# A 12-sublayer transformer kernel: L0X without its int16-to-bf16 cast, grouped attention with exponentials one step later, FFN heads merged, and the L3F Hadamard's last stage on TensorE

## The reference

```
        q = _fq_sym(q, axis=-1)          # k likewise; v along the keys
        attn = jnp.einsum('bhqd,bhkd->bhqk', q, k)
        attn = jax.nn.softmax(attn.astype(jnp.float32), axis=-1)
        attn = _fq_unsigned(attn, axis=-1)   # round(x / s) in 0..255, s = max / 255
        out = jnp.einsum('bhqk,bhkd->bhqd', attn, v)
```

```
        def weight_quant(w):
            scale = 1.0 / jnp.clip(jnp.mean(jnp.abs(w)), EPS)
            wq = jnp.clip(jnp.round(w * scale), -1.0, 1.0) / scale
        ...
        def h_bitlinear(x, w):   # fwht: Walsh-Hadamard over the 1024 features
            return jnp.einsum('bsh,oh->bso', act_quant(fwht(x)), weight_quant(w))
        intermediate = jax.nn.silu(bitlinear(x, w_gate)) * bitlinear(x, w_up)
        return h_bitlinear(intermediate, w_down)
```

## Time and profile before

| | us |
|---|---|
| Median of 3 runs (lowest, highest) | 3699.54 (3693.35, 3704.68) |
| The profiled execution, and its span | 3698.16, 3696.4 |
| TensorE busy | 3011.3 (81%) |
| VectorE busy | 2610.3 (71%) |
| ScalarE busy | 1861.4 (50%) |
| GpSimd busy | 469.7 (13%) |

### The profile page before, as it was taken

The page is one execution under the profiler, slowest core; times in us unless marked ns, Lnnn a source line. Parts: engine busy times, 40 slices in busy tenths (PEclk is TensorE's granted clock), DMA queues, the critical chain, the costliest instruction groups (busy, mean ns, idle before and its releaser), DMA issues. The chain is left out here.

```text
span 3696.4 us, 55018 instructions
## 1 busy us (share of the span) xinstructions
PE 3011.3 (81%) x16870; PEld 2203.5 (60%) x16888; DVE 2610.3 (71%) x8154; ACT 1861.4 (50%) x5724; POOL 469.7 (13%) x589
## 2 busy tenths in 40 slices
PE   7985564988999999775599855699999999998565
PEld 5653332756777778552277632377777777776354
DVE  4658887348888887668855589667667676775776
ACT  4546675115555555446522234466666666664232
POOL 0002111001111110221111100111111111111100
PEclk9996555989999999886699977799999999998577
DMA  1004555100000000101100131000000000000011
GB/s 61 2 9 91 102 105 119 56 15 1 1 1 1 1 1 1 43 33 20 43 1 1 48 117 29 23 1 1 1 1 1 1 1 1 1 1 36 3 23 43
DMA packets 192417, 96.23 MB, mean 26 GB/s; under 512 B 186112, under 2 KB 190336, under 8 KB 190464
## 3 DMA queue, kind: packets, MB, share of 16 engines
q1 hardware_dynamic: 192128, 92.73, 10.3%
HBM read 44.47 MB, written 2.10 MB: 13 GB/s over the span
## 5 line engine op out<-in xcount | busy, mean ns | idle before, releaser
L2269 ACT ACTIVATE L3A_probs<-L3A_masked,L3A_negmax 128x128 f32<-128x128 f32 (+1 forms) x512 | 229.3, 451 | 222.0 <-DVE L3A_negmax L2320 221.2
L336 PE MATMUL ps<-s_weights_b,s_XT 128*128 128x512 f32 (+1 forms) x640 | 300.7, 600 | 17.0 <-ACT s_XT L759 7.1
L2320 DVE CUSTOM_DVE_ANT_0 L3A_masked<-ps,L3A_hidden,L3A_negrstd 128x128 f32<-128x128 f32 (+1 forms) x512 | 193.7, 415 | 104.1 <-PE ps L2211 80.7
L2239 PE MATMUL ps<-s_weights_b,L3A_OT 128*128 128x256 f32 x1024 | 263.2, 380 | 0.0
L2192 POOL TENSOR_TENSOR L3A_rstd<-L3A_ve,s_mhalf 128x4 f32<-128x4 f32 x144 | 145.1, 1007 | 866.2 <-DVE L3A_ve L2152 866.2
L2176 DVE TENSOR_TENSOR L3A_rot<-ps,L3A_G 128x512 f32<-128x512 f32 x144 | 99.6, 692 | 207.4 <-ACT s_oT L2117 128.4
L885 ACT ACTIVATE L0X_pf<-ps,L0X_bias,L0X_qscale 128x512 int16<-128x512 f32 x256 | 197.0, 777 | 94.0 <-DVE L0X_bias L918 93.5
L336 PE MATMUL ps<-s_weights_b,s_Xc 128*128 128x512 f32 x512 | 241.3, 594 | 0.0
L915 DVE TENSOR_REDUCE L0X_negmax<-ps 128x2 f32<-128x1024 f32 x128 | 156.1, 1220 | 38.8 <-PE ps L826 38.5
L336 PEld LDWEIGHTS ps<-s_weights_b,s_XT 128*128 128x128 f32 x640 | 122.8, 211 | 101.5 <-issue 71.6
L2239 PEld LDWEIGHTS ps<-s_weights_b,L3A_OT 128*128 128x128 f32 x1024 | 175.4, 191 | 13.1
(11 more groups left out here) (510 smaller groups left out, 8298.8 us busy)
## 6 DMA issues: line engine op xcount, KB each, us to landing
s_weights_b<-w_L3A SPq DMA_DIRECT2D x1, 9984.0 KB, 26.8
s_weights_b<-w_L1A SPq DMA_DIRECT2D x1, 7936.0 KB, 21.5
s_weights_a<-w_L2F SPq DMA_DIRECT2D x1, 4224.0 KB, 12.8
s_weights_b<-w_L1F SPq DMA_DIRECT2D x1, 3840.0 KB, 12.1
s_weights_b<-w_L3F SPq DMA_DIRECT2D x1, 3136.0 KB, 11.3
s_weights_a<-w_L2A SPq DMA_DIRECT2D x1, 2898.0 KB, 10.5
s_weights_a<-w_L0F SPq DMA_DIRECT2D x1, 2176.0 KB, 9.8
s_X<-x SPq DMA_DIRECT2D x1, 2048.0 KB, 8.3
```

What stands on the lines that cost most here:

```text
L336: last = pe.matmul(out, lhs(k), rhs(k), start=(k == 0), stop=(k == n - 1))
L2239: last = pe.matmul(c.bank(3)[:, j * DM:(j + 1) * DM], OT[:, u % 4, j * P:(j + 1) * P], w["wo"][:, h, :], start=(h == 0 and j == 0), stop=( ...
L2269: last = a.activation(pr[:, u % 4, cols], ms[:, u % 2, cols], ACT.Exp, bias=nmx[:, h, j:j + 1], scale=-1.0, accum_out=sm[:, h, j:j + 1])
L2320: last = eng.tensor_tensor_reduce(out=ms[:, u % 2, cols], in0=s[:, cols], in1=hidden[:, P - j * P:2 * P], scale=-1.0 if gated else nrs[:, ...
```

## The change

**L0X.** The cast is gone. `pf` has four buffers, the DMA transpose reads it as it is, and PE reads the 16 bits of each whole number as a half-precision float: 0 to 255 are then subnormals, n times 2 to the -24. V is half precision too. A factor 2^-24 goes into the reciprocal of the sums (one more small DVE operation for each sequence). exps(p) now waits for the landing of transpose p-4, and `VALUE_LAG` is 5.

```
-    VALUE_LAG = 6
+    VALUE_LAG = 5
...
-        pf = S.sb("pf", [P, 3, 2, KEYS], I16)
-        ph = S.sb("ph", [P, 4, 2, KEYS], BF16)
-        pT = S.sb("pT", [P, 4, 2, KEYS], BF16)
+        pf = S.sb("pf", [P, 4, 2, KEYS], I16)
+        pT = S.sb("pT", [P, 4, 2, KEYS], I16)
...
-                        sp.wait_ge(vec_stepped, vec_steps(p))
+                    sp.wait_ge(exp_ready, p + 1)
                     if p >= 4:
                         sp.wait_ge(o_made, p - 3)
-                    sp.dma_start_transpose(out=pT[:, p % 4].rearrange("p x (t q) -> p (x t) q", q=P), in_=flat(ph[:, p % 4])).then_inc(
+                    sp.dma_start_transpose(out=pT[:, p % 4].rearrange("p x (t q) -> p (x t) q", q=P), in_=flat(pf[:, p % 4])).then_inc(
...
-                            last = pe.matmul(c.bank(6)[:, j * DM + h * DH:j * DM + (h + 1) * DH], pT[:, p % 4, x, t * P:(t + 1) * P],
+                            last = pe.matmul(c.bank(6)[:, j * DM + h * DH:j * DM + (h + 1) * DH], pT[:, p % 4, x, t * P:(t + 1) * P].bitcast(F16),
...
+                    if p >= 4:
+                        a.wait_ge(turned[p % 4], 16 * (p // 4))
...
-                    v(eng.reciprocal(ri[:], sm[:, b % 2]))
+                    v(eng.tensor_scalar(ri[:], sm[:, b % 2], STEP, None, ALU.mult))
+                    v(eng.reciprocal(ri[:], ri[:]))
...
-                    if 0 <= s - 2 < U and not by_pool(s - 2):
-                        steps_of(s - 2)
```

```
                         take_out(s - 5)
+                    if 0 <= s - 1 < U:
+                        exps(s - 1)
                     for x in early.get(s, []):
                         act_side(a, x)
                     if 0 <= s - 3 < U:
                         take_probs(s - 3)
-                    if 0 <= s < U:
-                        exps(s)
...
+                    if 0 <= s - 2 < U:
+                        normalize(s - 2)
                     if 0 <= s < U:
                         maxima(s)
-                    if 0 <= s - 1 < U:
-                        normalize(s - 1)
```

```
+                for m in (2, 1):
+                    a.activation(flat(Wb[2][:]), parts[m], ACT.Abs, accum_out=tot[:, m:m + 1]).then_inc(last_sums_ready, 1)
+                    a.wait_ge(last_sums_ready, 3 - m)
+                if norms:
+                    a.wait_ge(inv_ready, 1)
+                    a.activation(lnp[:, 0:3], mean[:, 0:3], ACT.Ln, bias=c.ones[:, 0:1]).then_inc(ln_ready, 1)
...
+                    prepare(0)
+                else:
+                    a.activation(warm[:], c.ones[:, 0:1], ACT.Silu)
...
+                    if s == 0:
+                        weights(1)
+                    if s == 2:
+                        weights(2)
```

```
-                    for ch in range(FCH):
-                        last = pe.matmul(c.bank(5 + ch // 4)[:, (ch % 4) * P:(ch % 4 + 1) * P], uT[:, ch, :], w["h128"],
-                                         start=True, stop=True)
+                    for ch in range(FCH // 2):
+                        two = c.bank(5 + ch // 2)[:, (ch % 2) * 2 * P:(ch % 2 + 1) * 2 * P]
+                        pe.matmul(two, uT[:, ch, :], hx[:, 0:2 * P], start=True, stop=False)
+                        last = pe.matmul(two, uT[:, ch + FCH // 2, :], hx[:, P:3 * P], start=False, stop=True)
...
-                    for s in (1, 2, 4):
+                    for s in (1, 2):
```

More of the change, by code:

```diff
@@ L1259, in sublayer_ternary_ffn @@
         hq_turned = S.sem("hq_turned_0", "hq_turned_1")
         parts = [flat(w["w1"]), flat(w["w2"]), flat(w["w3"])]
[L1261 to L1301, removed]
@@ L1302, in sublayer_ternary_ffn @@
-        S.clear()
+        warm = S.sb("warm", [P, 1])
+        nmagic = S.sb("nmagic", [P, 1])
+        count = 1.0 / (F1024 * DM)
         def row(t):
@@ L1457, in input_mean, with input_factor, weights @@
                     v(eng.tensor_scalar(ms[:, t, 0:1], ss[:, t, 0:1], 1.0 / DM, 1e-8, ALU.mult, ALU.add), xmean_ready)
+                def input_factor(t):
+                    b_ = am2[:, t, 0:XQ] if norms else am2[:, t, 0:1].to_broadcast([P, 2])
+                    v(eng.tensor_tensor(f[:, t, 0:2], b_, wsc[:, 0:2], ALU.mult))
+                def weights(m):
+                    part, out = parts[m], flat(Wb[m][:])
+                    if norms:
+                        eng.wait_ge(part_ready, m + 1)
+                        v(eng.tensor_scalar(out, part, MAGIC, MAGIC, ALU.add, ALU.subtract), w_ready, free=True)
+                    elif m == 2:
+                        eng.wait_ge(part_ready, 3)
+                        v(eng.tensor_scalar(out, out, -1.0, 1.0, ALU.max, ALU.min), w_ready, free=True)
+                    else:
+                        if m == 0:
+                            v(eng.tensor_scalar(part, part, inv[:, 0:1], MAGIC, ALU.mult, ALU.add))
+                        else:
+                            eng.wait_ge(part_ready, 1)
+                        v(eng.tensor_scalar(part, part, MAGIC, 1.0, ALU.subtract, ALU.min))
+                        v(eng.tensor_scalar(out, part, -1.0, None, ALU.max), w_ready, free=True)
                 def scale_input(t):
@@ L1569, in norm @@
                                         ALU.subtract, ALU.mult))
+                eng.wait_ge(S.loaded, 16)
+                v(eng.tensor_reduce(tot[:, 0:1], parts[0], AX.X, ALU.add, apply_absolute_value=True), sums_ready, free=True)
                 if norms:
                     input_mean(0)
+                else:
+                    v(eng.memset(nmagic[:], -MAGIC), free=True)
                 scale_input(0)
+                if hadamard:
+                    for k in range(2):
+                        v(eng.tensor_copy(hx[:, k * P:(k + 1) * P], w["h128"]), free=True)
+                    v(eng.tensor_scalar(hx[:, 2 * P:3 * P], w["h128"], -1.0, None, ALU.mult), free=True)
+                eng.wait_ge(sums_made, 1)
+                v(eng.tensor_scalar(mean[:, 0:3], c.bank(0)[:, 0:3], count, None, ALU.mult))
+                if norms:
+                    v(eng.tensor_scalar(wsc[:, 0:3], mean[:, 0:3], 1e-8, None, ALU.add))
+                else:
+                    v(eng.tensor_scalar(wsc[:, 0:3], mean[:, 0:3], 1e-5, None, ALU.max))
+                v(eng.reciprocal(inv[:, 0:3], wsc[:, 0:3]), inv_ready)
+                if norms:
+                    eng.wait_ge(ln_ready, 2)
+                    v(eng.tensor_tensor(wsc[:, 0:3], lnp[:, 0:3], lnm[:, 0:3], ALU.subtract))
+                    v(eng.tensor_scalar(wsc[:, 0:3], wsc[:, 0:3], 0.5 / levels, None, ALU.mult))
+                weights(0)
+                input_factor(0)
                 for s in range(NT + LAG + 1):
```

102 lines of the change are left out of this document (56 added, 46 removed).

## The result

The changed kernel takes 3635.01 us (median of 4 runs, 3634.05 to 3638.49), the kernel before beside it 3698.67: a ratio of 0.983, interval 0.981 to 0.985. That is 64 us less, where 39 were forecast, and 1 us outside the range. The profiled execution is the slowest of the four, 3638.49 us; its span is 59.7 us shorter than the one before.

| | before | after | difference | forecast |
|---|---|---|---|---|
| L0A | 259.6 | 261.9 | +2.3 | 0 |
| L0X | 364.6 | 343.7 | -20.9 | -22 |
| L1A | 686.0 | 675.8 | -10.2 | -5 |
| L1F | 179.5 | 175.7 | -3.8 | -4.5 |
| L2X | 95.2 | 99.5 | +4.3 | 0 |

What follows compares the result with a forecast made beforehand. It took TensorE to bound L3A, VectorE L0X, and a chain through TensorE and ScalarE L3F. Terms -22 - 5 - 26 - 16 + 30 = -39 took 3698.2 to 3659, 3660 as median; range 3636 to 3689 us.

Steps and rivals of the forecast that it cites:

- the stretch of seven pairs: L0X: 15.5 us of a sequence where TensorE waits for the turned queries' copy; no gain counted, to stay unchanged.
- paid by the slot that the cast no longer takes: L0X: one slot less of `VALUE_LAG` is offset by the removed cast's slot; no gain of its own counted.
- I count all 24.6: L3A: the new order removes all of TensorE's 31 waits for the copy `OT`, 24.6 us.
- Behind a full TensorE nothing further is to be had: L3A: no gain beyond the counted waits; some 25 us of gaps stay at its start and end.
- The slot of X: L1A and L3A: new slot sets TensorE's waits for X's copies beside other work; -5 in L1A, 1.4 more in L3A.
- The FFN heads: Starts of L2F, L3F and L1F: shorter path to the first Silu; -5.8, -5.9 and -4.5, sum -16 us.
- L3F's Hadamard: L3F: transform's doubled columns lengthen the ring through TensorE and ScalarE by 1.7 us a tile; +30, bounds +27 and +56.
- (a): L0X gives the whole cast, -43.5 in place of -22; some 3639 us; chance 0.12.
- (c): L0X gives nothing, since ScalarE and the queries' chain hold all of it; 3682 us; chance 0.11.
- (b): L3F: clock stays at 0.50 through the whole transform, +56 in place of +30; 3686 us; chance 0.14.
- (d): L3F: transform is hidden because a tile waits for VectorE; some 1 us gained per tile; 3614 us; chance 0.07.
- (e): L3A: turn(u) waits for normalize(u), 0.2 us at each of 256 heads, 50 us lost; above 3710; chance 0.06.

Runs made afterwards that it cites:

- the filled kernel: The changed kernel plus TensorE matmuls that compute nothing in L3F's waits: 3608.95 us; with L3F's old Hadamard as well (the one with VectorE at 88%): 3585.96 us.

## Why the prediction was wrong

- **L0X** met its number in part by luck: -20.9 for -22, a middle sequence of 39.1 us on average for 38.8, maxima 1.5 us apart, and the stretch of seven pairs as long as before (15.5 us). But the sum gave nearly all of the 22 to the cast and nothing to the lag: "paid by the slot that the cast no longer takes" is not what happened. The slot lets `outputs` go ahead of Q+; with the lag taken back L0X is only 13.5 us shorter than before (364.6 to 351.1). A cast put 8 us too high and a lag put at nothing, with 7, cancelled. The wait that the lag shortens stood in the trace of the kernel before and was not counted.
- **L3A is the step that failed**, by the size of a term. "I count all 24.6" and "Behind a full TensorE nothing further is to be had": the mechanism was right (the copy `OT` behind a stand of ScalarE), the term was mis-sized. The row of waits counts from the recorded end of a pipelined instruction; the same waits are worth 40.3 us, by taking the order back, or 43 for ScalarE's move alone. The busy 1003.6 us that the prediction took for work held 10 us of what the change won.
- **The slot of X** was mis-sized as well: 1.4 in L3A for a row sum of 5.4, because of a guess on where side work lies; taking it back cost 6.6 there and 6.2 in L1A. (The order's 40.3 and the slot's 6.6 are 2 us more than L3A gained; a kernel with both taken back was not run.)
- **L1A**: 6.2 of the slot and 3.4 of VectorE's order, which the prediction had not counted at all, make 9.6 of its -10.2.
- **The FFN heads** were right: with -6.3 in L2F and, by the kernel with the old Hadamard, 231.5 - 225.2 = 6.3 in L3F, and 3.8 in L1F with the extra table load in it, -16.4 for -16.
- **L3F's Hadamard** was right in sign and mechanism and 5 us too high: +24.6 for +30. The transforms took 5.2 us on average from start to start in place of 3.4, 30 us in all as forecast. That the mean met 5.2 is in part luck: the forecast took one course of the clock for all tiles, and they range from 3.56 to 6.56 us; another execution of the same code had 4.7 us less in them. But the down projection behind them ran at the higher clock more often (1.5 us a tile on average in place of 1.8 from start to start, 5 us in all). The prediction had named only the transform.
- **Rivals.** (a) and (c) did not come about, L0X gave half of the ceiling. (b) holds, nearly, in four of sixteen tiles. (d) is refuted by the unchanged waits of 2.33 and 1.10 us and by the filled kernel, where VectorE at 88% still does not hold. (e) is right in its mechanism and wrong in its size: turn does wait for normalize, at eight heads of 256, which the prediction had named as a sign of being wrong; it costs 2.7 us, not 50.

What stays open is what sets the 3 to 4 us by which L0A, L2A, L2X and L3A, and the up to 6 us by which L3F, differ between executions of the same code.

## What to carry to other kernels

Where an engine is pipelined, price a wait from the start of the instruction ahead to the start of the one behind, less the pitch that the same pair has without it; the row of waits was 27 us where 40 were to be had, and a wait of 0.29 us, eight times in L3A, was in no row. If an undone wait should give more than the idle time, look whether the busy time of the same instruction count falls. When a sum comes out right, take its parts back one by one: here a lag that was counted at nothing was worth a third of L0X's gain. Before moving work from an engine with room to one in the ring, find out at which clock the ring runs: here keeping TensorE at work in its waits gave 27 us, more than any move of the Hadamard.

## What the runs showed of the hardware

- A matmul's recorded length is not its cost: transposes recorded at 0.27 us start 0.11 us apart, and the first matmul behind a wait took 0.50 us to the next in place of 0.43.
- TensorE reads int16 whole numbers as half-precision subnormals without a penalty that shows: the values' matmuls of L0X, the ones whose type changed, start 0.027 us apart (median) in both kernels, and TensorE is busy 206.6 us for 1664 instructions where it was 205.3.
- The granted clock in L3F rose from 0.79 (3387 to 3626 us) to 0.92 (3384 to 3595 in the filled kernel) when TensorE had useless work in its waits, and the sublayer became 28 us shorter. The same transform of 16 instructions took 3.56 us at the higher level and up to 6.56 mostly at the lower.
- Two profiled executions of a single kernel differed by 3 to 4 us in each of three sublayers, with a granted clock of 0.75 in one and 0.84 in the other at the start of L2X.
